# A decoder layer on one core: context keys and values folded in three f32r passes, the value fold spread over four array quarters, and calls reordered

## The reference

```python
x = x + attn(_layernorm(x), w_qkv, ln_w, w_proj)      # 16 heads of 8, causal in groups of 32 tokens
x = x + xattn(_layernorm(x), context, gamma, beta, w_q, w_kv, w_out, b_out, gate)
x = x + ffn(_layernorm(x), router_w, ...)             # 16 experts, top 4, and 2 shared ones

def xattn(x, context, ...):
    xn = _layernorm(x, gamma, beta)
    q = xn @ w_q                                      # 16 heads of 64
    k, v = split(context @ w_kv)                      # this product is what the change computes anew
    attn = softmax((q * 64 ** -0.5) @ k.T)
    return ((attn @ v) @ w_out + b_out) * tanh(gate)
```

## Time and profile before

| | |
|---|---|
| median of three runs | 188.43 us (188.37 to 188.70) |
| the profiled execution: its own time | 188.91 us |
| its span, first to last instruction | 187.2 us, so 1.71 us lie around the span |
| TensorE matmuls busy | 175.6 us (94%) |
| VectorE busy | 139.7 us (75%) |
| GpSimd busy | 120.7 us (64%) |
| ScalarE busy | 107.4 us (57%) |
| granted TensorE clock | 1.000 over the whole span |

### The profile page before, as it was taken

How to read it: one execution, slowest core, us unless ns; L and a number is a source line. 1 busy time by engine, 2 the same in 40 slices (tenths; PEclk the granted TensorE clock), 3 DMA queues, 4 the chain that set the end, 5 groups by cost and what they waited for, 6 DMA issues and landing times.

```text
span 187.2 us, 4577 instructions
## 1 busy us (share of the span) xinstructions
PE 175.6 (94%) x1685; PEld 133.3 (71%) x1685; DVE 139.7 (75%) x308; ACT 107.4 (57%) x211; POOL 120.7 (64%) x178
## 2 busy tenths in 40 slices
PE   5999999999899989998999999999999999999992
PEld 5798776667666657778778675766677888888881
DVE  5767595868968987899989869982277667775665
ACT  6378768667666553564595394344255666555540
POOL 4473899815465786966555502038999999998700
PEclk9999999999999999999999999999999999999999
DMA  5977510000001000220000002719976554400003
GB/s 141 268 240 207 157 33 5 2 4 4 4 2 29 0 18 14 57 69 4 2 0 0 4 2 79 208 50 278 364 219 175 164 160 157 127 7 0 2 0 112
DMA packets 17718, 15.75 MB, mean 84 GB/s; under 512 B 2224, under 2 KB 13568, under 8 KB 17568
## 3 DMA queue, kind: packets, MB, share of 16 engines
q1 hardware_dynamic: 16832, 15.13, 27.6%
q10 hardware_dynamic: 864, 0.33, 0.6%
HBM read 14.86 MB, written 0.59 MB: 83 GB/s over the span
## 4 chain that ended last, share of the span: by engine, by line
PE 74%; DVE 12%; POOL 6%; issue 4%; ACT 3%; DVEq 0%; POOLq 0%; ACTq 0%
PE banks L1718 6%; PE banks L1783 5%; PE banks L1744 5%; PE banks L1765 5%; PE banks L1767 4%; PE banks L1766 4%; PE banks L1768 4%; PE banks L1770 4%; PE banks L1769 4%; PE banks L1704 3%; PE banks L1675 3%; PE banks L1787 3%; PE banks L1788 3%; PE banks L1786 3%; PE banks L1689 2%
## 5 line engine op out<-in xcount | busy, mean ns | idle before, releaser
L865 ACT ACTIVATE s<-banks 128x512 f32<-128x512 f32 x36 | 21.4, 599 | 31.1 <-PE banks L1767 31.0
L526 POOL TENSOR_TENSOR act<-act,vbd 128x512 f32<-128x512 f32 x14 | 22.2, 1586 | 1.9 <-DVE act L1324 0.8
L715 POOL TENSOR_TENSOR gu_lo<-gu_w,gu_hi 128x256 fp32r<-128x256 f32 x14 | 11.2, 800 | 16.4 <-ACT gu_hi L871 16.4
L1324 DVE TENSOR_TENSOR act<-s,banks 128x512 f32<-128x512 f32 x20 | 13.7, 685 | 10.2 <-ACT s L865 8.8
L526 POOL TENSOR_TENSOR qk_fold<-qk_fold,vbd 128x512 f32<-128x512 f32 x12 | 19.2, 1607 | 0.8 <-DVE qk_fold L1324 0.4
L1324 DVE TENSOR_TENSOR qk_fold<-s,banks 128x512 f32<-128x512 f32 x16 | 10.9, 686 | 9.9 <-PE banks L1770 6.7
L1765 PE MATMUL banks<-x3hi,gu_lo 128*128 128x512 f32 x36 | 17.7, 490 | 0.2 <-POOL gu_lo L715 0.2
L1744 PE MATMUL banks<-vo_fold,p2T 128*128 128x128 f32 x128 | 16.6, 279 | 1.2 <-ACT p2T L859 1.1
L535 POOL TENSOR_SCALAR ve<-mv 128x1 f32<-128x1 f32 x16 | 3.2, 197 | 22.0 <-DVE mv L1106 21.8
L1744 PEld LDWEIGHTS banks<-vo_fold,p2T 128*128 128x128 f32 x128 | 15.3, 192 | 2.6 <-ACT p2T L859 2.0
L518 POOL TENSOR_TENSOR kbd<-kbd,rs 128x1024 f32<-128x1024 f32 x8 | 15.2, 1902 | 2.4 <-DVE rs L1208 2.3
(11 more groups left out here) (177 smaller groups left out, 467.5 us busy)
## 6 DMA issues: line engine op xcount, KB each, us to landing
vbd<-comb_rows SPq DMA_DIRECT2D x30, 256.0 KB, 3.7
wkv_sb<-in_L_xattn_w_kv_dram SPq DMA_DIRECT2D x1, 1024.0 KB, 8.2
gu_w<-in_L_ffn_gate_w_dram SPq DMA_DIRECT2D x16, 64.0 KB, 2.2
gu_w<-in_L_ffn_up_w_dram SPq DMA_DIRECT2D x16, 64.0 KB, 3.3
vo_fold<-in_L_ffn_down_w_dram SPq DMA_DIRECT2D x1, 960.0 KB, 6.5
wq_sb<-in_L_xattn_w_q_dram SPq DMA_DIRECT2D x1, 512.0 KB, 6.2
wout_sb<-in_L_xattn_w_out_dram SPq DMA_DIRECT2D x1, 512.0 KB, 6.5
x<-in_x_dram SPq DMA_DIRECT2D x3, 128.0 KB, 2.9
```

What stands on the lines that cost most here:

```text
L526: engine.tensor_tensor(act_of(k), act_of(k), spread[:, j % SPREAD, :], ALU.mult).then_inc(scale_early if j < RING else scale_s, 1)
L865: sc.activation(sil[:, k % 2, :], bank[2 * (k % 2)], ACT.Silu).then_inc(sil_s, 1)
L1324: dve.tensor_tensor(act_of(k), sil[:, k % 2, :], bank[2 * (k % 2) + 1], ALU.mult).then_inc(g_s, 1)
```

## The change

Three things.
1. `("kv", j)` takes split operands. ScalarE rounds the context (`ctx_hi`, in place of `ctxT`) and the weights (`round_kv(q)`, four calls, each for two pairs) to f32r. The rests are made by VectorE (`rest_ctx`, `rest_kv` for q = 0, 1) and GpSimd (`rest_kv` for q = 2, 3). TensorE adds up three products per output in place of one float32 product. The split parts lie in buffers that only later stages use.
2. In `("VW", j)` four products in a row now go to the four different row and column halves, and the unit waits for both halves of its banks before its first product.
3. The hand-written lists are reordered on all engines, up to the thirteenth gate and up unit.

The diff, cut to its core:

```diff
@@ buffers
-        ctxT = sb("ctxT", [P, B, CTX])
+        ctx_hi = x3hi[:, 4 * P:4 * P + B * CTX]
+        ctx_lo = x3lo[:, 4 * P:4 * P + B * CTX]
+        kvw_hi = [act_hi[:, 0, :], act_hi[:, 1, :], act_hi[:, 2, :], x3hi[:, 0:4 * P]]
+        kvw_lo = [act_lo[:, 0, :], act_lo[:, 1, :], act_lo[:, 2, :], x3lo[:, 0:4 * P]]
@@ new calls
+        def kv_weights(q):
+            return wkv_sb[:, :].rearrange("p (m j d) -> p j m d", m=2, j=NPAIR)[:, 2 * q:2 * q + 2, :, :]
+        def rest_kv(engine, q):
+            engine.wait_ge(kvhi_s, q + 1)
+            engine.tensor_tensor(kvw_lo[q].rearrange("p (j m d) -> p j m d", j=2, m=2), kv_weights(q),
+                                 kvw_hi[q].bitcast(F32).rearrange("p (j m d) -> p j m d", j=2, m=2),
+                                 ALU.subtract).then_inc(kvlo_s if q < 2 else kvlo_p, 1)
+            def round_kv(q):
+                sc.wait_ge(wkv_l, 16)
+                sc.copy(kvw_hi[q].rearrange("p (j m d) -> p j m d", j=2, m=2), kv_weights(q)).then_inc(kvhi_s, 1)
+            def rest_ctx():
+                dve.wait_ge(f_copied, unit_no[("ctx", 0)] + 1)
+                dve.tensor_tensor(ctx_lo, bank[7][:, 0:B * CTX], ctx_hi.bitcast(F32), ALU.subtract).then_inc(clo_s, 1)
@@ fold, kind kv
-                    pe.wait_ge(wkv_l, 16)
+                    if j == 0:
+                        pe.wait_ge(clo_s, 1)
+                    if j < 4:
+                        pe.wait_ge(kvlo_s, j // 2 + 1)
+                    else:
+                        pe.wait_ge(kvlo_p, j // 2 - 1)
...
+                    hi, lo = kvw_hi[j // 2], kvw_lo[j // 2]
                     for m in range(2):
-                        last = pe.matmul(bank[min(fold_banks(u))][:, m * B * CTX:(m + 1) * B * CTX],
-                                         wkv_sb[:, m * INNER + j * P:m * INNER + (j + 1) * P],
-                                         ctxT[:, :, :].rearrange("p b s -> p (b s)"), start=True, stop=True)
+                        dst = bank[min(fold_banks(u))][:, m * B * CTX:(m + 1) * B * CTX]
+                        cols = slice((j % 2 * 2 + m) * P, (j % 2 * 2 + m + 1) * P)
+                        pe.matmul(dst, lo[:, cols], ctx_hi, start=True, stop=False)
+                        pe.matmul(dst, hi[:, cols], ctx_lo, start=False, stop=False)
+                        last = pe.matmul(dst, hi[:, cols], ctx_hi, start=False, stop=True)
@@ fold, kind VW
-                    for h in range(2):
-                        if h == 0:
-                            pe.wait_ge(half_s, NPAIR // 2 + j)
-                        else:
-                            pe.wait_ge(f_copied, copies_before(u, {FOLD + h}))
-                        hs = slice(DH * h, DH * (h + 1))
-                        for b in range(B):
-                            bs = slice(b * CTX, (b + 1) * CTX)
-                            for pair, c in ((2 * j, h), (2 * j + 1, 1 - h)):
+                    pe.wait_ge(half_s, NPAIR // 2 + j)
+                    pe.wait_ge(f_copied, copies_before(u, {FOLD + 1}))
+                    for b in range(B):
+                        bs = slice(b * CTX, (b + 1) * CTX)
+                        for swap in range(2):
+                            for h in range(2):
+                                hs = slice(DH * h, DH * (h + 1))
+                                pair, c = (2 * j + 1, 1 - h) if swap else (2 * j, h)
                                 last = pe.matmul(bank[FOLD + h][CTX * c:CTX * (c + 1), b * D:(b + 1) * D],
                                                  kv_sb[hs, pair, 1, bs], wout_sb[hs, pair, :], start=True, stop=True)
@@ ScalarE's list (one place of several)
             copy_xnT(2)
+            round_kv(0)
             copy_q(1)
             copy_fold(("wq", 0))
             copy_v(0)
@@ VectorE's list
             sum_squares(1)
+            rest_kv(dve, 0)
             norm_apply_pair(3)
@@ stage three: VectorE's, then ScalarE's list
+            choose_experts(early)
             multiply(1)
             split_x3(6)
-            choose_experts(early)
...
             silu(5)
+            round_weights(5)
             silu(6)
-            round_weights(5)
@@ GpSimd's list: rest_kv(2) and rest_kv(3) stand among the first splits of
   the down weights; split_weights 1, 2 and 3 move behind norm_p2 1, 2 and 4
+            rest_kv(pool, 2)
+            split_down(1)
+            rest_kv(pool, 3)
```

More of the change, by code:

```diff
@@ L201, in decoder_layer @@
         wkv_l = sem("wkv_loaded")
+        kvhi_s = sem("kv_weights_hi")
+        kvlo_s = sem("kv_weights_lo")
+        kvlo_p = sem("kv_weights_lo_by_pool")
+        clo_s = sem("ctx_lo")
         wout_l = sem("wout_loaded")
@@ L659, in _ @@
             split_down(4)
+            norm_scale(1, 0)
             split_down(5)
@@ L684, in _ @@
             norm_apply(1, 7)
-            split_weights(2, 2, 0)
             norm_p2(pool, 1)
+            split_weights(1, 1, 0)
             norm_scale(2, 0)
@@ L689, in _ @@
             norm_p2(pool, 2)
-            split_weights(3, 3, 0)
+            split_weights(2, 2, 0)
             norm_scale(2, 1)
@@ L698, in _ @@
             norm_apply(2, 3)
+            split_weights(3, 3, 0)
             norm_p2(pool, 5)
@@ L816, in copy_fold @@
                 if kind == "ctx":
-                    sc.copy(ctxT[:, :, :].rearrange("p b s -> p (b s)"), bank[7][:, 0:B * CTX]).then_inc(f_copied, 1)
+                    sc.copy(ctx_hi, bank[7][:, 0:B * CTX]).then_inc(f_copied, 1)
                 elif kind == "wq":
@@ L931, in _ @@
             copy_xnT(3)
+            round_kv(1)
             copy_v(1)
@@ L938, in _ @@
             copy_v(2)
+            round_kv(2)
+            round_kv(3)
             copy_v(3)
@@ L1006, in _ @@
             copy_x3T(3)
+            exp2(6)
             exp_logits(early)
-            exp2(6)
             copy_p2T(5)
@@ L1031, in _ @@
             copy_combT(1)
+            round_weights(6)
             silu(10)
-            round_weights(6)
             round_weights(7)
@@ L1352, in _ @@
             normalize_k(2)
+            rest_kv(dve, 1)
             sum_squares(3)
@@ L1360, in _ @@
             max1_sub(1)
+            mask1(2)
             norm_y(0)
-            mask1(2)
+            max1_sub(2)
             residual1(0)
-            max1_sub(2)
+            norm_stats(1, 0)
             norm_y(1)
-            norm_stats(1, 0)
             mask1(3)
+            max1_sub(3)
             residual1(1)
-            max1_sub(3)
             norm_stats(1, 1)
@@ L1374, in _ @@
             max1_sub(4)
+            mask1(5)
             norm_y(3)
             norm_stats(1, 2)
-            mask1(5)
             max1_sub(5)
@@ L1437, in _ @@
             norm_stats(2, 7)
+            choose_experts(early)
             multiply(1)
             split_x3(6)
-            choose_experts(early)
+            multiply(2)
             split_x3(7)
-            multiply(2)
             expert_weights(early)
@@ L1474, in _ @@
             multiply(8)
+            multiply(9)
             scale_act(dve, 1)
-            multiply(9)
+            multiply(10)
             scale_act(dve, 2)
-            multiply(10)
             scale_act(dve, 3)
@@ L1851, in _ @@
             project_v(3)
+            scores1(1)
             fold(("kv", 2))
-            scores1(1)
             fold(("kv", 3))
@@ L1856, in _ @@
             fold(("A", 0))
+            scores1(2)
             values1(0)
             fold(("kv", 4))
+            transpose_p1(1)
             transpose_y(0)
-            scores1(2)
-            transpose_p1(1)
+            fold(("kv", 5))
             project_out(0)
-            fold(("kv", 5))
+            scores1(3)
             values1(1)
@@ L1866, in _ @@
             transpose_y(1)
-            scores1(3)
             transpose_p1(2)
@@ L1873, in _ @@
             transpose_y(2)
+            scores1(4)
             transpose_p1(3)
-            scores1(4)
             project_out(2)
             fold(("kv", 7))
+            values1(3)
             scores1(5)
-            values1(3)
             fold(("A", 3))
+            scores1(6)
             transpose_y(3)
             transpose_p1(4)
+            project_out(3)
             fold(("VW", 0))
-            project_out(3)
-            scores1(6)
             values1(4)
+            scores1(7)
+            transpose_y(4)
             transpose_p1(5)
-            transpose_y(4)
-            scores1(7)
             project_out(4)
@@ L1892, in _ @@
             values1(5)
+            transpose_p1(6)
             fold(("VW", 1))
-            transpose_p1(6)
             transpose_y(5)
@@ L1900, in _ @@
             fold(("VW", 2))
+            transpose_p1(7)
             transpose_y(6)
-            transpose_p1(7)
             project_out(6)
+            fold(("x2", 2))
             scores2(1)
-            fold(("x2", 2))
             values1(7)
@@ L1933, in _ @@
             output2(3, 1)
+            transpose_p2(4)
+            scores2(7)
             logits(2)
```

(14 more changed lines are left out.)

52 lines of the change are left out of this document (25 added, 27 removed).

## The result

The changed kernel takes 188.18 us (median of 17 runs, 187.47 to 188.79), the kernel before 188.79 beside it (17 runs): ratio 0.9967, 95% interval 0.9955 to 0.9978. It is 0.6 us faster where 3.1 were forecast, and outside the range. The part around the span, which the forecast took as fixed at 1.71, is 1.9 on average.

A forecast was written before the change was run, and what follows sets the result against it. TensorE was three quarters of the chain of waits, with VectorE binding stage two beside it. Terms of +0.3, -0.6, -0.55, -0.65, -1.2, -0.2 and -0.2 gave -3.1, so 185.4 us, range 184.0 to 187.3.

The forecast's parts named there:

- Start: First 25 us: roundings and rests of the split operands, queued behind the weights' landing, cost +0.3; bounds 0 and +0.7.
- Kv units: TensorE's folds of keys and values: a unit falls from 0.96 to 0.82 us, together -0.6.
- the four units counted: Keys and values units from ("kv", 4) on, held to lie on the path: 4 x 0.14 = 0.6.
- Rival 4: TensorE's keys and values folds: a 256-column f32r pass costs 0.24 like one of 512; slower, 189.5 us; chance 0.08.
- Waits for the fold's copy and late scores: Stage one's new order: two of three TensorE waits for fold copies go, -0.55; earlier scores of tiles 6 and 7, -0.65.
- VW: TensorE's value folds, four products at a time: a unit falls from 1.52 to 0.9 us; units 0 and 1 -1.2, others -0.2.
- units 2 and 3: Late VW units on TensorE, said to be hidden behind VectorE's list before residual1(7): 0.2 in all.
- Rival 2: VW folds on TensorE: row halves don't run together, the 1.4 of VW is gone, 186.8 us; chance 0.08.
- Rival 3: Helpers are the new bound: ScalarE's late start +0.4 more, VectorE's subtractions beside GpSimd +1.4; 187.2 us; chance 0.12.
- The rival's other half: ScalarE's late start at the kernel's beginning, taken in full: +0.4 more than the forecast's +0.3.
- Stage two: gate_up(0) before transpose_p2(5) and split_weights(3) before norm_p2(5) swap equal lengths: 0; bounds -0.5 and +0.5, with stage three.
- Stage three: round_weights(5) before silu(6) removes the 0.23 us for which gate_up(7) waited: -0.2.

The follow-up runs named there:

- load_in_two: Changed kernel with the wkv load as two transfers, the first units' columns first, and the first rounding waiting for that part alone: ratio 0.9943, 187.53 us.
- no_kv: Changed kernel with the keys and values units back in float32 and without roundings and rests (new order and new VW stay): ratio 0.9949.
- all_new: Changed kernel with wkv loaded in two transfers, split_weights(3) behind norm_p2(3) and round_weights(5) behind silu(6), new second stage kept: ratio 0.9937.
- round023_later: Changed kernel with three of ScalarE's wkv roundings moved behind the path's work, nothing else moved: ratio 1.0198, 3.7 us slower.
- first_unit_later: Changed kernel with the first kv unit's whole chain (ScalarE's rounding, VectorE's rest, TensorE's unit) moved behind the path's work: ratio 1.0045.

## Why the prediction was wrong

Measured against the forecast's terms, in the order of its sum, each by the columns:

- **Start: "I take +0.3", "Part is absorbed".** The failed step: it measured +1.15 in the profile. The place, the wait and what is queued behind it were named. But the landing was taken as the 12.4 of one trace and came at 12.8, it moves by about a microsecond between executions, and nothing was absorbed by `scores1(0)`. 1.0 is the wait (`load_in_two`; 0.5 on average over the runs), the rest the roundings. Bounds 0 to +0.7 were too narrow because they held one sample of a load.
- **Kv units, -0.6.** Right: -0.7 (33.36 to 32.65), of which 0.6 comes at the four units counted. It was -0.5 in the old order and -0.9 beside `no_kv`. Rival 4 falls: six passes with a load each, all on all rows, start 0.12 apart. With it falls here the rule in the list of the Trainium skill, "TensorE: Matmul & The Clock Gate", under "What overlaps and what doesn't", by which I estimated 0.21. The rests cost less than I said, 0.69 on VectorE for 0.83.
- **Waits for the fold's copy and late scores, -1.2; VW, -1.4.** Together -2.0 of the -2.6, and singly wrong: -0.4 each. The order alone gave a third of its 1.2. VW gave 1.6 with the order and 0.4 without, because of the joint wait that I named and priced at nothing; and units 2 and 3, which I called hidden (0.2), gave 0.97 of the 1.6. That the two errors partly cancel is luck. VW's units took 1.04 where I said 0.9. Rival 2 falls: row halves and column halves do run together.
- **Rival 3, VectorE beside GpSimd, 1.4.** Not charged, and rightly: `residual1(7)` came 8.03 us after `softmax2_max(0)`, where I said 8.3 to 8.5. Three of its eight subtractions are long, 1.70, 1.10 and 0.82 us, but three were before (1.18, 1.17 and 0.93), so that 0.3 us was added and not 1.4. The rival's other half, ScalarE's late start in full, came true and more: `softmax2_max(0)` came at 55.09 where I said 53.6.
- **Stage two, "change places with work of equal length: 0".** The second failed step, +0.73. I judged a call by its own length, not by who is queued behind it. `split_weights(3)` (1.34 us) in front of `norm_p2(5)`, and the maxima of S2(6) (2.4 us) in front of the sum over P2(5), both hold the norm that `transpose_p2(5)` needs. Behind it, small VectorE operations fell beside GpSimd's next norm.
- **Stage three, "takes away the 0.23 ... -0.2".** The third failed step: wrong sign, +0.43. I named who waits for the rounding and not who is released by it. An earlier rounding releases GpSimd's split, which fell on VectorE's smallest operations.

In sum 0.85 + 0.73 + 0.63 us for the three, and 0.3 for the stretch between: 2.5, the distance from -3.1 to -0.6. That it comes out to the tenth holds for the two profiled executions, and the start among them scatters by 0.4.

## What to carry to other kernels

A helper that must wait for a load should not stand in front of path work on an in-order engine, and when it must, the load is cut so that the part needed first lands with time to spare: the landing in one trace is a sample, not a date. When a call is moved, price what is queued behind it and what it releases, not its length. And judge a reordering by stretches between fixed calls; totals hid here that two causes of 0.7 us each covered the other, so that undoing either alone left the stage as long. And two waits joined into one are paid at the later of the two: what fills that time decides whether the faster unit is worth 0.4 us or 1.6.

## What the hardware showed that I had not expected

- Two VectorE operations with two inputs on 128x4 took 0.80 us in place of 0.23, one of them 719 ns for 158, when a GpSimd operation of 0.77 us began at the same time, 113.86. The Trainium skill, "SBUF — State Buffer", under "SBUF: two separate sides", has the later one of a VectorE operation with two inputs in SBUF and a GpSimd operation that reads it blocked for the whole instruction; this case's trace agrees, also for operations with almost nothing to move: VectorE's pair ended at 114.66, GpSimd's operation at 114.63. A VectorE operation with one input, on 128x64, took 1.72 us in `all_new` in place of 0.25, beside GpSimd's norm of 1.90.
- TensorE's granted clock, 1.00 all through the kernel before, was 0.73 over 3 us in `round023_later` after TensorE had stood idle for 2.4 us, and passes in it started 0.21 us apart in place of 0.12; two waits of 1.5 us in `first_unit_later` left it at 1.00.
- Six f32r passes of 256 columns on 128 rows start, after the first, 0.11 to 0.12 us apart with a fresh 128-column weight load each.
- The same 1024 KB load, issued at the same place, let ScalarE begin at 11.3, 12.2, 12.8 or 13.0 us in four traces.
- The time around the span is 1.7 to 1.8 us in every run of the kernels without the kv split, and from 1.7 to 2.8 in those with it. Why is open.
